# First attention of a fused four-stage kernel: other places for silu, the value scaling and two squares

## The reference, cut to what matters

```python
qg = split_heads(tokens @ Wqg, HEADS)            # 16 heads
kv = split_heads(tokens @ Wkv, HEADS)
queries, gates = (qg[..., :DIM_KEYS], qg[..., DIM_KEYS:])   # 16 and 64 wide
keys, values = (kv[..., :DIM_KEYS], kv[..., DIM_KEYS:])
queries, keys, values = (l2norm(queries), l2norm(keys), l2norm(values))
sim = jnp.einsum('bhid,bhjd->bhij', queries, keys)
attn = jnp.square(jax.nn.relu(sim))
aggr = jnp.einsum('bhij,bhjd->bhid', attn, values)
out = tanh_norm(aggr) * jnp.tanh(jax.nn.silu(gates))
return out @ Wout                                 # heads put side by side first
```

## Time and profile before

| | |
|---|---|
| median of 3 runs | 1910.02 us (1909.36 to 1914.42) |
| the profiled execution | 1913.23 us, span 1911.6 us |
| busy over the span | PE 65%, DVE 61%, POOL 50%, ACT 38% |
| granted TensorE clock, mean | 0.77 |
| the phase of this change | 360 to 1230 us of the span, about |

### The profile page before, as it was taken

One profiled execution on the slowest core, in us unless ns is written; L12 is line 12 of the kernel. 1 busy time (PEld: TensorE's weight loads), 2 busy tenths in 40 slices (PEclk: granted clock), 3 DMA queues, 4 the chain that ended last, 5 costly groups with the idle time before them and its releaser, 6 DMA issues.

```text
span 1911.6 us, 28781 instructions
## 1 busy us (share of the span) xinstructions
PE 1246.5 (65%) x8794; PEld 793.2 (41%) x8795; DVE 1167.8 (61%) x2728; ACT 720.8 (38%) x1238; POOL 946.6 (50%) x1112
## 2 busy tenths in 40 slices
PE   3435324366877777777778776547777777756886
PEld 1223212234554444544455454413333333325775
DVE  6788851166666666676666765257777777743332
ACT  1101002154444444444444443126565555532221
POOL 2356576555555555645555533333454445425554
PEclk8555555578888888888888888758888888878676
DMA  4010004300000000000000000030000000001110
GB/s 130 23 25 14 13 13 93 80 6 1 7 8 8 6 6 6 0 6 6 6 6 6 7 4 4 14 91 12 18 15 11 16 17 14 8 17 42 43 40 12
DMA packets 73501, 40.93 MB, mean 21 GB/s; under 512 B 23956, under 2 KB 68861, under 8 KB 73429
## 3 DMA queue, kind: packets, MB, share of 16 engines
q1 hardware_dynamic: 50674, 24.02, 4.5%
q0 software_dynamic: 20384, 11.67, 3.0%
q10 hardware_dynamic: 2370, 4.35, 0.8%
HBM read 31.12 MB, written 23.87 MB: 29 GB/s over the span
## 4 chain that ended last, share of the span: by engine, by line
PE 38%; DVE 29%; issue 12%; POOL 9%; ACT 6%; DMA 3%; ACTq 1%; POOLq 0%; SPq 0%; DVEq 0%
PE psum L1143 5%; PE psum L1164 4%; DVE terms L1801 4%; POOL xe_dram L569 4%; PE psum L1278 3%; PE psum L1153 3%; PE psum L1207 3%; DVE attn L1628 3%; PE psum L1196 2%; PE psum L1225 2%; PE psum L1187 2%; DVE q_highT L1827 2%; DVE newton L1616 2%; POOL out L777 2%; PE psum L1301 1%
## 5 line engine op out<-in xcount | busy, mean ns | idle before, releaser
L1801 DVE TENSOR_REDUCE terms<-psum 128x4 bf16<-128x1024 f32 x128 | 156.9, 1226 | 54.1 <-PE psum L1301 53.1
L855 ACT ACTIVATE attn<-psum 128x1024 f32<-128x1024 f32 x128 | 130.5, 1020 | 156.9 <-PE psum L1126 156.7
L630 POOL DMA_INDIRECT yg<-ye_dram,routel x128 | 142.4, 1112 | 41.3 <-issue 33.0
L950 ACT ACTIVATE prob<-psum 128x512 f32<-128x512 f32 x256 | 139.4, 601 | 44.0 <-PE psum L1265 42.6
L1143 PE MATMUL psum<-attn,v 128*64 128x256 f32 x1024 | 147.8, 412 | 6.2 <-POOL attn L610 4.3
L569 POOL DMA_INDIRECT xe_dram<-rows_out,route x128 | 131.7, 1029 | 39.6 <-issue 39.3
L1207 PE MATMUL psum<-x3T,w_g 128*128 128x256 f32 x256 | 93.5, 528 | 82.3 <-DVE silu_g L1738 80.8
L1164 PE MATMUL psum<-ident,o_factor 128*64 128x128 f32 x1024 | 88.4, 345 | 78.5 <-DVE silu_g L1738 58.2
L1628 DVE TENSOR_TENSOR attn<-attn 128x1024 f32<-128x1024 f32 x80 | 127.4, 1593 | 0.8 <-issue 0.8
L1164 PEld LDWEIGHTS psum<-ident,o_factor 128*64 128x64 f32 x1024 | 79.1, 179 | 97.9 <-DVE silu_g L1738 64.9
L610 POOL TENSOR_TENSOR attn<-attn 128x1024 f32<-128x1024 f32 x48 | 92.6, 1929 | 28.9 <-ACT attn L855 28.6
(11 more groups left out here) (302 smaller groups left out, 3219.0 us busy)
## 6 DMA issues: line engine op xcount, KB each, us to landing
x4n_dram<-x4n SPq DMA_DIRECT2D x16, 256.0 KB, 3.8
w<-in_w POOLq DMA_DIRECT2D x48, 64.0 KB, 2.4
x_in<-in_x SPq DMA_DIRECT2D x8, 256.0 KB, 2.7
xe_dram<-zero_rows SPq DMA_DIRECT2D x8, 256.0 KB, 3.3
x_dram<-x1s SPq DMA_DIRECT2D x8, 256.0 KB, 2.4
xe_dram<-rows_out,route POOLq DMA_INDIRECT x128, 2.1
xe<-xe_dram SPq DMA_DIRECT2D x16, 128.0 KB, 2.4
ye_dram<-ye SPq DMA_DIRECT2D x16, 128.0 KB, 2.0
```

The costliest lines, as they stand in the source:

```text
L630: pool.indirect_dma_start(yg[fetch.p][:, j, k, :], None, ye_dram, bass.IndirectOffsetOnAxis(ap=where[:, j, K0 + k:K0 + k + 1], axis=0), bo ...
L855: act.activation(r[:], psum[:, 2 * (g % 2):2 * (g % 2) + 2, :], ACT.Relu).then_inc(s["relu_made"], 1)
L950: act.activation(prob[place % 8][:], bank[place % 3][:], ACT.Exp, scale=SCALE).then_inc(s["exp_made"], 1)
L1801: dve.tensor_reduce(dst[:, :, 2 * m2:2 * m2 + 2], psum[:, 4:6, :].rearrange("q p (b k) -> q p b k", b=2), AX, ALU.max, negate=True).then_i ...
```

## The change

Four edits, all in the third phase:

1. On DVE, the silu of the gates' first two halves goes from g = 4, behind the Newton turns and the scaling of `qk`, to g = 3, ahead of the Newton turns. The Newton turns and the scaling go to the start of g = 4, and the silu of the second two halves comes right behind the scaling, where before a product with the gate and a square of `attn` stood between.
2. On POOL, the scaling of the values waits for the scaled `qk` and no longer for the inverse roots.
3. On DVE, at g = 5, the tail's two products `oT` come first, then the square of pair 4 (before at the start of g = 5), then the split of the terms.
4. The squares of pairs 2 and 6 go from POOL to ACT, each right behind its own relu, with a wait for it. Pair 3 stays with POOL.

```diff
--- before.py
+++ after.py
@@ -340,11 +340,12 @@
             s[name] = sems(name)
         for name in ("x2_made qk_squared qk_copied v_squared v_copied "
                      "sq_reduced g_tanh silu_made gate_made qk_scaled high_made terms_made terms_ps qkT_act qkT_dve inv_made v_made "
-                     "score_ps relu_made attn_made attn_made_pool attn_read aggr_sq_made aggr_out norm_ps o_norm_made o_len_made o_tanh_made "
+                     "score_ps relu_made attn_made attn_made_pool attn_made_act attn_read aggr_sq_made aggr_out norm_ps o_norm_made o_len_made o_tanh_made "
                      "o_factor_made factor_ps o_made y3T_ps y3T_made y3_ps x3_made yg_cleared phases").split():
             s[name] = sem(name)
         ring = [bank[6], bank[7]]
-        POOL_PAIRS = (2, 3, 6)
+        POOL_PAIRS, ACT_PAIRS = (3,), (2, 6)
+        DVE_PAIRS = (0, 1, 4, 5, 7)
 
 
         scope.pop().close()
@@ -643,19 +644,16 @@
                         hold(s["x2_made"], fetch.n - 2)
                     hold(s["routel_landed"][fetch.p], 16 * fetch.k)
                     gather(fetch, PLACES[0:5])
-                if att:
-                    square(att, POOL_PAIRS[0])
                 if tail:
                     length_of(tail, 1)
                 if att:
-                    square(att, POOL_PAIRS[1])
+                    square(att, POOL_PAIRS[0])
                 if fetch:
                     gather(fetch, PLACES[5:])
                 if tail:
                     factor(tail, 1)
                 if front:
-                    hold(s["inv_made"], front.n)
-                    hold(s["v_copied"], 4 * front.n)
+                    hold(s["qk_scaled"], front.n)
                     vv = v[front.p][:].rearrange("q j (h d) -> q (j h) d", d=DV)
                     pool.tensor_tensor(vv, vv, inv3[:, 4 * HEADS:].unsqueeze(2).to_broadcast([P, 2 * HEADS, DV]), ALU.mult).then_inc(s["v_made"], 1)
                 if fetch:
@@ -664,7 +662,6 @@
                     chain.need(n)
                     pool.tensor_tensor(rstd3[:], veps3[:], minus_half[:, 0:2], ALU.pow).then_inc(s["rstd3"], 1)
                 if att:
-                    square(att, POOL_PAIRS[2])
                     length_of(att, 0)
                 if fetch or att or tail:
                     chain.restart()
@@ -853,6 +850,9 @@
                 wait(act, s["attn_read"], PAIRS * (att.n - 1) + g + 1 - RING)
                 act.wait_ge(s["score_ps"], PAIRS * (att.n - 1) + g + 1)
                 act.activation(r[:], psum[:, 2 * (g % 2):2 * (g % 2) + 2, :], ACT.Relu).then_inc(s["relu_made"], 1)
+                if g in ACT_PAIRS:
+                    act.wait_ge(s["relu_made"], PAIRS * (att.n - 1) + g + 1)
+                    act.activation(r[:], r[:], ACT.Square).then_inc(s["attn_made_act"], 1)
 
             def square_of(front, k, src):
 
@@ -1133,10 +1133,9 @@
                     wait(pe, s["aggr_out"], 4 * (q.n - 1) + b - 1)
                 if g == 0:
                     pe.wait_ge(s["v_made"], q.n)
-                if g in POOL_PAIRS:
-                    pe.wait_ge(s["attn_made_pool"], len(POOL_PAIRS) * (q.n - 1) + POOL_PAIRS.index(g) + 1)
-                else:
-                    pe.wait_ge(s["attn_made"], (PAIRS - len(POOL_PAIRS)) * (q.n - 1) + g - sum(x < g for x in POOL_PAIRS) + 1)
+                for who, name in ((POOL_PAIRS, "attn_made_pool"), (ACT_PAIRS, "attn_made_act"), (DVE_PAIRS, "attn_made")):
+                    if g in who:
+                        pe.wait_ge(s[name], len(who) * (q.n - 1) + who.index(g) + 1)
                 for c in range(2):
                     for h in range(2):
                         head = 2 * g + h
@@ -1691,11 +1690,17 @@
                 chain.need(n)
                 dve.sem_inc(s["terms_made"], 1)
 
+            def silu(front, b):
+                m = 4 * (front.n - 1) + b + 1
+                wait(dve, s["gate_made"], 2 * (front.n - 2) + b // 2 + 1)
+                dve.wait_ge(s["g_tanh"], m)
+                dve.scalar_tensor_tensor(silu_g[b // 2][:, 512 * (b % 2):512 * (b % 2) + 512], tanh_g[b % 2][:], 1.0, ring[b % 2][:], ALU.add, ALU.mult).then_inc(s["silu_made"], 1)
+
             def half(fetch, front, att, tail):
                 for g in range(PAIRS):
                     if g == 0 and tail:
                         square(tail, PAIRS - 1)
-                    if g > 0 and att and g - 1 not in POOL_PAIRS:
+                    if g > 0 and att and g - 1 in DVE_PAIRS and g != 5:
                         square(att, g - 1)
                     if front and g == 0:
                         for j in range(2):
@@ -1723,26 +1728,25 @@
                     if front and g == 3:
                         v_sum(front, 2)
                         v_sum(front, 3)
+                        silu(front, 0)
+                        silu(front, 1)
+                    if front and g == 4:
                         dve.wait_ge(s["sq_reduced"], 6 * front.n)
                         inverse_root(inv3[:], norm3[:], 6 * HEADS, s["inv_made"])
                         qk3 = qk[:].rearrange("q j h d -> q (j h) d")
                         dve.wait_ge(s["inv_made"], front.n)
                         dve.tensor_tensor(qk3, qk3, inv3[:, 0:4 * HEADS].unsqueeze(2).to_broadcast([P, 4 * HEADS, DK]), ALU.mult).then_inc(s["qk_scaled"], 1)
-                    if front and g in (4, 5):
-                        for h in range(2):
-                            b = 2 * (g - 4) + h
-                            m = 4 * (front.n - 1) + b + 1
-                            wait(dve, s["gate_made"], 2 * (front.n - 2) + g - 3)
-                            dve.wait_ge(s["g_tanh"], m)
-
-                            dve.scalar_tensor_tensor(silu_g[g - 4][:, 512 * h:512 * h + 512], tanh_g[h][:], 1.0, ring[h][:], ALU.add, ALU.mult).then_inc(s["silu_made"], 1)
+                        silu(front, 2)
+                        silu(front, 3)
                     if att and g == 4:
                         gate_aggregate(att, 0)
-                    if front and g == 5:
-                        split_terms(front)
                     if tail and g == 5:
                         scale_output(tail, 2)
                         scale_output(tail, 3)
+                    if att and g == 5:
+                        square(att, 4)
+                    if front and g == 5:
+                        split_terms(front)
                     if fetch and g == 5:
                         combine(fetch)
                     if att and g == 6:
```

## The result

The changed kernel takes **1844.66 us** (median of 4 runs, 1840.37 to 1851.23); the ratio to the kernel before is 0.9656, 95% interval 0.9618 to 0.9694. 1842 us were forecast. The profiled execution took 1840.37 us (span 1838.7 us, mean granted clock 0.786), against 1913.23 us before.

What follows compares the result with a forecast made beforehand. PE's waits for DVE were taken to set the step, some paid twice through half clock. 15 steps at 4.7 us make 70, less 1 or 2 given back: -69, giving 1842 us; 8 in 10 range 1806 to 1876.

Steps and rivals of the forecast that it cites:

- The gates: PE's gates' second half: the 5.22 us wait for silu goes, eight matmuls take 1.89 us at full clock; PE 7.0 us ahead.
- The spread: PE's spreading of the tail's factor: still waits 3.7 us, takes 3.6 at half clock; next scores 4.9 us ahead.
- The square and the terms: Behind the spread: PE waits 1.6 us for pair 4's square; DVE makes the terms at 693.6, before at 695.70.
- The projection and the end of the step: Projection starts 3.0 us ahead, norms 3.5; the rest may gain 1.4 at full clock; 4.4 us for this step.
- a projection above 3.8 us: Sign of being wrong, on PE's output projection, which took 3.72 us before.
- The 0.3 us added for a mean step: Whole step: 4.7 us gained in a mean one, not 4.4, since this one waited only 2.12 us at the spread, mean 4.06.
- The value scaling: On POOL, from 686.3 to 689.8: 3.5 us, not 4.70; costs PE's chain nothing; 2.2 us gained on DVE's split.
- ACT's squares: Two squares moved from POOL to ACT: 1.0 us each, plus 0.1 waiting for its own relu, costed at nothing.
- Full clock everywhere: Rival, chance 0.13: factor not late, PE never at half clock, spread 1.7 us better; 7 us a step, 1805 us.
- POOL as the bound: Rival at the spread, chance 0.13: gathers held by DVE's turns, factor 2 us later; 2 us a step gained, 1880 us.
- slower: Rival, chance 0.05: value scaling holds pair 4's square up to 3.5 us, later PE work at half clock; 1966 us.
- nothing: Rival, chance 0.05: DVE, not PE, sets the step, and PE's waits only change places; 1910 us.

## Why the prediction was right

**The gates.** Right. The wait of 5.22 went, the gates ran at full clock (2.00 us for eight; 1.9 forecast).

**The spread.** Right: a wait of 3.7 and a spread of 3.6 were forecast, 3.60 and 3.63 measured. The third gather was held (1.43 us, where 1.00 and 1.99 were the bounds); the other two, beside Newton's short instructions, took 1.13 and 1.01. The factor, made at 660.61, came last, 0.53 us behind the one silu that the spread's first bank needs. The profile's row names silu, whose second instruction ended at 660.68; but with the factor made earlier the wait fell to 2.93 us. The 4.06 of before, beside which the 3.7 was put, was the mean of two kinds of step, which the prediction did not see.

**The square and the terms.** Right: PE waited 1.65 us for the square (1.6 forecast), and the terms were made 15.1 us after PE was free for the gates (668.31 - 653.18; forecast 693.6 - 678.29 = 15.3).

**The projection and the end of the step.** Here a term was mis-sized. The projection was taken at its old 3.72 us; it took 5.61, partly at half clock, and its start was 0.3 us later than worked out, since the turn ahead of it took 1.86 at half clock. The prediction let half a clock follow on the wait ahead of the spread, and had none for the turn and the projection. Whether the short waits of 1.65 and 1.06 us brought it is not shown: with the whole of edit 1 alone there were such waits too, and the projection took 3.72. By the prediction's own list a projection above 3.8 us was a sign of being wrong; that one sign came, while the others came as for right. The norms thus came at 22.9 us behind the gates' start, not at 21.1. In return they and the rest of the step ran at full clock: 5.55 us from the norms on, where it took 7.18 before, and 6.3 by the forecast (7.18 less 4.4 - 3.5). In the end the step gained 4.39 us in the mean, not 4.7; over 15 steps that is 5 us less. That it came so near is in part luck. The step shown was to gain 4.4 us; from the gates to the last scores it took 28.5 us, not 27.4, and was 31.8 before, so it gained 3.4. The middle step gained 3.7 (51.51 - 47.79). The mean is higher because two of the 13 steps before took 53.5 us and three of the 13 now 46.0 to 46.6, of which the prediction knew nothing. The 0.3 us added for a mean step had no ground either: the steps of before with the long wait at the spread took no longer than the others. In the profiled execution the third phase, from its first combination to its last x3, went from 857.9 to 793.2 us: 64.7 less, 69 forecast. The other 8 us between the two executions lie in phases that the change doesn't touch.

**The value scaling.** Right in size (3.5 forecast, 3.62 measured) and in place (it starts 7.4 us behind the gates, 8.0 forecast). Its wait is without effect, as the run with the old one showed. But to count its gain only as the split's 2.2 us was too short: what matters is where the square and the split stand beside it, and the runs showed that with the value scaling moved away the old order is 47 us faster than the new one (1843.81 - 1796.39), which the prediction did not see.

**ACT's squares.** Right: 1.06 us, at no cost.

**The attribution.** The forecast put the gain on silu's first pair, and the run with it alone won 65 us (1910.00 - 1845.18). That edits 2 to 4 give nothing holds only beside edit 1; alone they give 24 us.

**The rivals.** Full clock everywhere did not come, since the wait at the spread stayed. POOL as the bound, slower, and nothing did not come either. The first two were each seen in part in a kernel of their own (Newton started earlier; the factor early), not in this one. The range of 8 in 10, 1806 to 1876, was said to take in the first rival and most of the second, but their own times, 1805 and 1880, lie just outside it.

## What to carry to other kernels

Edits around one wait don't add up, so try them alone and in pairs: here moving the value scaling won nothing in one order of DVE's work and 53 us in the other (1849.02 - 1796.39). When a long POOL instruction and DVE's two-operand instructions share a stretch, look for a stretch where DVE idles or reads PSUM, before trading their order (in the changed kernel DVE's product with an operand in PSUM took 0.68 us beside the value scaling). A wait removed ahead of one clock fall may only move the fall, as from the gates to the projection here: look at the granted clock of every later piece too.

## What the runs showed of the hardware

**The port is not given by the recorded start.** With only the first silu pair moved, DVE's square began at 665.98 by its record, and POOL's value scaling at 666.54; still the square ended only 1.1 us behind the scaling. POOL's gather, factor and scaling stood back to back, and DVE did not get in between. The Trainium skill ("SBUF — State Buffer", section "SBUF: two separate sides") says that whichever starts first gets the shared pair for the whole instruction. The stretched square agrees with the lock, but not with "first" by the recorded starts.

**How long a gather was held.** A POOL gather took 1.00 us in the step of the earlier trace rows. In the changed kernel the third one (658.93, 1.43 us) ended 0.87 us behind the scaling of `qk` (658.26, 1.23 us), in the earlier trace rows the second one ended 0.88 behind it (425.44 + 1.99 against 425.33 + 1.22), and with the factor early one (663.25, 1.63) ended 0.89 behind it (662.77, 1.22). So the longer the scaling still had to run when the gather came, the longer the gather took.

**Steps of one length.** In the changed kernel, in those with edit 2, 3 or 4 undone, in that with the factor early, in that with the value scaling last and the new order, and in that with the first silu pair alone, most steps take 47.5 to 48.0 us, although the spread waits 3.60 us in one and 8.78 in another, and the projection takes 5.61 or 3.72. Between these two the 5.2 us lost ahead of the spread came back by the projection's end, about half as a fuller clock (turn and projection 2.7 us shorter) and half as shorter waits (2.3 us). Why they meet so closely is open, and so is what sets the step. To take one wait out of such a loop need not show in the time.
